# A linear attention's drain written out in an order of its own, with other banks for its output projections and a layer norm over two batches

## The reference

```
q = silu(causal_dwconv(h @ Wq, taps of 4)); k likewise        # h: layer-normed x
q, k = layernorm per head of 128, times weight, plus bias
v = h @ Wv; beta = sigmoid(h @ Wb + bb); gate = silu(h @ Wg)
per token t:  S = (1 - b_t) * S + b_t * (v_t outer k_t);  o_t = S q_t
x = x + (o * gate) @ Wo
x = x + ffn(layernorm(x))        # router, top 2 of 8, two silu layers, sums to rows 0..7
```

## Time and profile before

| what | value |
|---|---|
| runs | 1192.81, 1193.85, 1196.03 us, median 1193.85 |
| the profiled execution's own time | 1192.82 us |
| its span, first to last instruction | 1190.9 us |
| TensorE busy | 1132.6 us (95%) |
| VectorE, ScalarE, GpSimd busy | 929.5 (78%), 773.4 (65%), 635.5 us (53%) |
| mean granted clock of TensorE | 0.98 of 2.4 GHz |
| linear attention's drain | 1104 to 1148 us |
| last feed-forward layer | 1148 to 1190.9 us |

### The profile page before, as it was taken

How to read it: one execution, slowest core, us unless ns; L and a number is a source line. 1 busy time by engine, 2 the same in 40 slices (tenths; PEclk the granted TensorE clock), 3 DMA queues, 4 the chain that set the end, 5 groups by cost and what they waited for, 6 DMA issues and landing times. The chain is left out here.

```text
span 1190.9 us, 22446 instructions
## 1 busy us (share of the span) xinstructions
PE 1132.6 (95%) x7558; PEld 910.8 (76%) x7558; DVE 929.5 (78%) x2126; ACT 773.4 (65%) x1535; POOL 635.5 (53%) x1077
## 2 busy tenths in 40 slices
PE   8999999887998899999999999999999999999768
PEld 7443434336667799999999999999999999999646
DVE  6788887846558888888888888888888888888552
ACT  3367777673456777776777776777676777676423
POOL 4020500000705776877786777686777687767520
PEclk9899999998999999999999999999999999999889
DMA  6434434400220112112111110211110201010020
GB/s 182 55 55 56 55 55 56 55 2 6 110 69 20 49 33 82 34 47 68 47 33 48 67 48 32 83 32 48 67 48 32 83 32 47 32 48 33 16 71 1
DMA packets 23449, 60.50 MB, mean 51 GB/s; under 512 B 3367, under 2 KB 8359, under 8 KB 22183
## 3 DMA queue, kind: packets, MB, share of 16 engines
q1 hardware_dynamic: 23335, 59.07, 19.3%
HBM read 44.67 MB, written 2.33 MB: 39 GB/s over the span
## 5 line engine op out<-in xcount | busy, mean ns | idle before, releaser
L1714 DVE SCALAR_TENSOR_TENSOR ln_xn<-l_proj_q,par,ln_xn 128x511 f32<-128x511 f32 (+2 forms) x192 | 142.8, 744 | 98.5 <-ACT ln_xn L1613 96.2
L689 DVE TENSOR_REDUCE a_neg_max<-a_scores 128x1 f32<-128x512 f32 x244 | 155.1, 684 | 36.6 <-PE a_scores L417 34.8
L608 ACT ACTIVATE a_probs<-a_scores_t 128x512 f32<-128x512 f32 x256 | 138.5, 600 | 62.8 <-PE a_scores_t L436 61.8
L1619 ACT ACTIVATE ln_xn<-ln_xn,par 128x512 f32<-128x512 f32 x128 | 92.6, 723 | 92.6 <-DVE ln_xn L1714 92.6
L1370 POOL TENSOR_TENSOR l_k_tok<-l_normed,k_norm 128x384 f32<-128x384 f32 x64 | 65.1, 1017 | 156.6 <-ACT l_normed L1630 156.6
L1714 DVE SCALAR_TENSOR_TENSOR ln_xn<-l_proj_k,par,ln_xn 128x511 f32<-128x511 f32 (+2 forms) x192 | 143.4, 747 | 4.5
L1630 ACT ACTIVATE l_normed<-l_turn_q,l_shift,l_scale 128x128 f32<-128x128 f32 x256 | 96.3, 457 | 25.8 <-POOL l_shift L1362 25.8
L1360 POOL TENSOR_TENSOR l_scale<-l_small,l_minus_half 128x8 f32<-128x8 f32 x64 | 105.1, 1642 | 5.0
L1630 ACT ACTIVATE l_normed<-l_turn_k,l_shift,l_scale 128x128 f32<-128x128 f32 x256 | 97.1, 480 | 0.0
L1684 ACT ACTIVATE l_gate<-l_proj_gv 128x512 f32<-128x512 f32 x64 | 38.2, 597 | 80.7 <-PE l_proj_gv L1432 80.7
L1568 PE MATMUL l_outp<-l_masked,l_values 128*128 128x128 f32 x512 | 89.6, 277 | 0.1
(11 more groups left out here) (347 smaller groups left out, 3618.6 us busy)
## 6 DMA issues: line engine op xcount, KB each, us to landing
l_keep<-keep_rows SPq DMA_DIRECT2D x64, 448.0 KB, 3.6
a_stack<-a_dense SPq DMA_DIRECT2D x90, 128.0 KB, 5.1
head_raw<-w_heads SPq DMA_DIRECT2D x8, 1024.0 KB, 6.7
x_tok<-x SPq DMA_DIRECT2D x4, 512.0 KB, 8.6
wo_raw<-w_o SPq DMA_DIRECT2D x1, 2048.0 KB, 11.2
out<-x_tok SPq DMA_DIRECT2D x1, 1920.0 KB
a_stack<-a_max_rows_t SPq DMA_DIRECT2D x64, 4.0 KB
ctx_tok<-w_qkv SPq DMA_DIRECT2D x1, 768.0 KB, 7.0
```

The costliest lines, as they stand in the source:

```text
L608: act.activation(probs[:, n % 2, h, :], scores_t[(4 * n + h) % TURNS][:], ACT.Exp, scale=SOFT_SCALE).then_inc(probs_done, 1)
L689: dve.tensor_reduce(neg_max[:, g % 2, at:at + 1], max_bank(g, j), AX.X, ALU.max, negate=True).then_inc(max_done, 1)
L1619: act.activation(conv[:, w, m, :], conv[:, w, m, :], ACT.Silu, bias=par[:, h, 2 * TAPS + w:2 * TAPS + w + 1]).then_inc(act_sem[w], 1)
L1714: ins = dve.scalar_tensor_tensor(conv[:, w, m, s:], proj[w][:, 0:SEQ - s], par[:, h, tap:tap + 1], conv[:, w, m, s:], ALU.mult, ALU.add)
```

## The change

The steps for u = 0 to 63 keep their order and lose their conditions; stages that the drain needs become functions (`score_unit`, `sum_chunks`, `read_state`, `project_out`, `copy_state`, `add_out`, `token_statistics`, `mask`, `gate_out`, `decays`, and on GpSimd `late_rows` is split into `scaled_keys`, `decayed_queries` and `shifted_keys`). The drain's further steps are replaced on each engine by a function `drain`, a list in an order of its own. Token turns of unit 63 write `proj_q` and `proj_k` instead of the turn banks. Output projections of units 59, 60, 61 and 63 write `proj_gv`, that of unit 62 `scores`, instead of `outp`. The layer norm's work for batch 2 ends in the drain with its deviations; normalise, transposes, high and low parts of batch 2 are left to the feed-forward layer, as (3, 2) says.

```diff
+        LAST = UNITS - 1
+
+        def turn_bank(v, w):
+
+            return proj[w] if v == LAST else turn[w]
+
+        def out_bank(v):
+
+            if v < UNITS - 5:
+                return outp
+            return scores if v == LAST - 1 else proj_gv
...
+            def drain():
+                rows_in = 16 * NB * PAIRS
+                gated_low(LAST - 3, BODY - 4)
+                scaled_keys(LAST - 1)
+                scales(LAST, BODY - 1)
+                ln_d.deviations(pool, 0)
+                decayed_queries(LAST - 1, BODY - 2, rows_in)
+                shifted_keys(LAST - 1)
+                decayed(LAST - 1, BODY - 2)
+                scaled_keys(LAST)
+                shifted_keys(LAST)
+                decayed(LAST, BODY - 1)
+                gated_low(LAST - 2, BODY - 3)
+                decayed_queries(LAST, BODY - 1, rows_in)
+                ln_d.deviations(pool, 1)
+                gated_low(LAST - 1, BODY - 2)
+                gated_low(LAST, BODY - 1)
+                ln_d.deviations(pool, 2)
+
+            steps(step)
+            drain()
...
                 wait(pe, act_sem[w], v + 1)
-                wait(pe, qk_ready[w], v)
+                if v < LAST:
+                    wait(pe, qk_ready[w], v)
                 for t in range(TPB):
-                    last = pe.transpose(turn[w][:, t * P:(t + 1) * P], conv[:, w, k % 2, t * P:(t + 1) * P], ident[:])
+                    last = pe.transpose(turn_bank(v, w)[:, t * P:(t + 1) * P], conv[:, w, k % 2, t * P:(t + 1) * P], ident[:])
...
+            def read_state(v, k, sums, gates):
+
+                m, e, c = k % 2, k % 2, k // 2
+                wait(pe, masked_done, v + 1)
+                wait(pe, state_done, v + 1)
+                wait(pe, q_decayed, v + 1)
+                wait(pe, values_done, v + 2 - k % 2)
+                wait(pe, added, sums)
+                wait(pe, gated_done, gates)
...
+            def project_out(v, k, head):
+
+                w, half, bank = k // 2, k % 2, out_bank(v)
+                wait(pe, gated_lo_done, v + 2 - half)
+                for t in range(2):
+                    tok, j = slice((half * 2 + t) * P, (half * 2 + t + 1) * P), 0
+                    for e in range(2):
+                        r = (2 * w + e) % 4
+                        for lhs, rhs in split_passes(gated_hi[:, r, tok], gated_lo[:, r, tok],
+                                                     wo_hi[:, head + e, :], wo_lo[:, head + e, :]):
+                            last = pe.matmul(bank[:, t * D:(t + 1) * D], lhs, rhs, start=(j == 0), stop=(j == 5))
+                            j += 1
+                last.then_inc(out_done, 1)
...
                 if has(u, 5):
-                    v, kk = u - 5, (k - 5) % BODY
-                    w, half = kk // 2, kk % 2
-
-
-                    wait(pe, gated_done, min(v + 3, UNITS) if isinstance(v, int) else v + 3)
-                    wait(pe, gated_lo_done, v + 2 - kk % 2)
+
+                    v = u - 5
+                    wait(pe, gated_done, v + 3)
...
+            def drain():
+                head = 2 * (PAIRS - 1)
+                for w in range(2):
+                    turn_tokens(LAST, BODY - 1, w)
+                for w in range(2):
+                    turn_back(LAST - 1, w)
+                wait(pe, values_done, UNITS)
+                project_out(LAST - 4, BODY - 5, head)
+                score_unit(LAST - 1, BODY - 2)
+                read_state(LAST - 2, BODY - 3, LAST - 4, 0)
+                turn_back(LAST, 0)
+                sum_chunks(LAST - 1, BODY - 2)
+                turn_back(LAST, 1)
+                score_unit(LAST, BODY - 1)
+                ln_d.transpose(pe, 0, proj)
+                read_state(LAST - 1, BODY - 2, 0, LAST - 1)
+                sum_chunks(LAST, BODY - 1)
+                wait(pe, added, LAST - 3)
+                project_out(LAST - 3, BODY - 4, head)
+                read_state(LAST, BODY - 1, 0, LAST)
+                wait(pe, added, LAST - 2)
+                project_out(LAST - 2, BODY - 3, head)
+                ln_d.transpose(pe, 1, proj)
+                wait(pe, masked_done, UNITS)
+                project_out(LAST - 1, BODY - 2, head)
+                wait(pe, added, LAST - 1)
+                project_out(LAST, BODY - 1, head)
+
+            steps(step)
+            drain()
...
+            def drain():
+                gated_high(LAST - 3, BODY - 4)
+                norm_affine(LAST - 1, BODY - 2, 0)
+                norm_affine(LAST - 1, BODY - 2, 1)
+                normalise(LAST, BODY - 1, 0)
+                normalise(LAST, BODY - 1, 1)
+                copy_state(LAST - 1, BODY - 2)
+                norm_affine(LAST, BODY - 1, 0)
+                norm_affine(LAST, BODY - 1, 1)
+                gated_high(LAST - 2, BODY - 3)
+                ln_d.high_parts(act, 0, proj)
+                copy_state(LAST, BODY - 1)
+                gated_high(LAST - 1, BODY - 2)
+                gated_high(LAST, BODY - 1)
+                ln_d.high_parts(act, 1, proj)
+
+            steps(step)
+            drain()
...
+            def add_out(v, k):
+                n = batch_of(v) * TPB + 2 * (k % 2)
+                wait(dve, out_done, v + 1)
+                wait(dve, added, v - 2)
+                dve.tensor_tensor(x_tok[:, n:n + 2, :], out_bank(v)[:].rearrange("p (t d) -> p t d", t=2),
+                                  x_tok[:, n:n + 2, :], ALU.add).then_inc(added, 1)
...
-                if u in (UNITS + 2, UNITS + 4):
-                    ln_d.low_parts(dve, (u - UNITS - 2) // 2, proj)
-                if u in (UNITS + 1, UNITS + 3):
-                    ln_d.normalise(dve, (u - UNITS - 1) // 2)
-                if u in (UNITS, UNITS + 2, UNITS + 4):
-                    wait(dve, added, UNITS - BODY + 2 * ((u - UNITS) // 2 + 1))
-                    ln_d.statistics(dve, (u - UNITS) // 2)
...
+            def drain():
+                add_out(LAST - 5, BODY - 6)
+                token_statistics(LAST, BODY - 1)
+                wait(dve, added, UNITS - BODY + 2)
+                ln_d.statistics(dve, 0)
+                mask(LAST - 1, BODY - 2)
+                gate_out(LAST - 2, BODY - 3)
+                ln_d.normalise(dve, 0)
+                add_out(LAST - 4, BODY - 5)
+                decays(LAST, BODY - 1, 16 * NB * PAIRS)
+                carry(LAST - 1, BODY - 2)
+                mask(LAST, BODY - 1)
+                gate_out(LAST - 1, BODY - 2)
+                wait(dve, added, UNITS - BODY + 4)
+                ln_d.statistics(dve, 1)
+                carry(LAST, BODY - 1)
+                add_out(LAST - 3, BODY - 4)
+                ln_d.low_parts(dve, 0, proj)
+                gate_out(LAST, BODY - 1)
+                ln_d.normalise(dve, 1)
+                add_out(LAST - 2, BODY - 3)
+                wait(dve, added, UNITS - BODY + 6)
+                ln_d.statistics(dve, 2)
+                ln_d.low_parts(dve, 1, proj)
+                add_out(LAST - 1, BODY - 2)
+                add_out(LAST, BODY - 1)
 
             dve.wait_ge(consts_set, 2)
-            steps(step, 7)
-            ln_d.low_parts(dve, NB - 2, proj)
+            steps(step)
+            drain()
...
+        norm_and_ffn(nc, semaphore, "d", ffn, xn_hi, xn_lo, ident, x_tok, norm_tiles, ln_d, (NB - 1, NB - 2), out=out)
 
 
 def kernel(**inputs):
```

More of the change, by code:

```diff
@@ L1301, in has, with steps @@
             return not isinstance(u, int) or 0 <= u - lag < UNITS
-        def steps(step, lags):
+        def steps(step):
             for pair in range(PAIRS):
@@ L1330, in step @@
                     sp.dma_start(w_raw[:], w_heads[bass.ds(pair + 1, 1)]).then_inc(w_loaded, 16)
-            steps(step, 0)
+            steps(step)
         @block.gpsimd
@@ L1418, in step @@
                     low_weights(pair, of, k - SPLIT_AT[0])
-            steps(step, 4)
-            for g in range(1, NB - 1):
-                ln_d.deviations(pool, g)
+            def drain():
[18 more added lines that the diff above has]
+            drain()
         @block.tensor
@@ L1503, in expert_rows, with score_unit, sum_chunks @@
                 last.then_inc(rows_done, 1)
+            def score_unit(v, k):
+                for w in range(2):
+                    wait(pe, qk_ready[w], v + 1)
+                wait(pe, masked_done, v)
+                for t in range(TPB):
+                    last = score(t, k % 2)
+                last.then_inc(scored, 1)
+            def sum_chunks(v, k):
+                wait(pe, state_done, v)
+                wait(pe, k_decayed, v + 1)
+                wait(pe, values_done, v + 2 - k % 2)
+                for t in range(LATER):
+                    last = pe.matmul(chunks[:, t * DK:(t + 1) * DK], k_tok[:, t, :],
+                                     values[:, k // 2 % 2, t, k % 2 * DK:(k % 2 + 1) * DK], start=True, stop=True)
+                last.then_inc(chunks_done, 1)
@@ new lines, in read_state @@
+            def read_state(v, k, sums, gates):
```

(41 more changed lines are left out.)

180 lines of the change are left out of this document (61 added, 119 removed).

## The result

The changed kernel takes 1182.3 us (median of 5 runs, 1178.67 to 1184.77) where the kernel before takes 1193.66 in the runs beside it (5 runs, 1191.56 to 1196.03): a ratio of 0.9899, 95% interval [0.9873, 0.9925]. The forecast was 1181.8. A second series gave 1181.2, ratio 0.9911 [0.9882, 0.994]. The profiled execution took 1182.66 us with a span of 1180.8, so the span is 10.1 us shorter than before, where the sum said 12.0; the medians differ by 11.4.

The account below looks back on a forecast made before the run. The drain was taken as bound by a chain hopping between engines, the rest by TensorE. Gains 0.3 + 10.3 + 1.4 = 12.0 us took 1192.82 to 1180.8, plus 1.0 for the median: 1181.8 us, range 1177.5 to 1186 (8 in 10).

Parts of the forecast that it names:

- (a): Drain start: unit 63's token turns go first, so GpSimd's scales end at 1112.0 us, 2.4 us earlier.
- (b): GpSimd's queue behind the scales: chunk sums of unit 62 at 1116.0, head start eaten; VectorE's normalise collision costs 0.4 us.
- (c): TensorE's hole, 1110.1 to 1116.0: clock falls, back between 1119 and 1126; gain to unit 62's gate 0.3 us with (b).
- (d): Drain after the gate multiply of unit 62: chain of 11.5 us instead of 21.8, gain 10.3 us.
- (e): Feed-forward layer: batch 2's transposes cost 1.02 us, starting at the high clock gains 2.4; net gain 1.4 us.
- The bank waits: Old drain: TensorE's projections waited 1.9 and 1.8 us for the shared bank `outp`; these were to leave the chain.
- Rival 3: Drain not bound by order: new waits replace old ones one for one, time within 0.3%; chance 0.03.
- Rival 1: No low clock in the drain: gate of unit 62 2.5 to 3 us better, 1179 us; chance 0.15.
- rival 4: Slower: the hole leaves TensorE at 1.2 GHz for good, 1212 us; chance 0.03.
- Rival 2: GpSimd's queue replaces the bank; with longer low clock, gain 6 to 9 us, 1185 to 1188 us; chance 0.13.

Follow-up runs that it names:

- e6: Changed kernel with 52 unused identity transposes added on TensorE to fill its hole; 1179.03 us, ratio to the kernel before 0.9889.
- e7: Changed kernel with VectorE's normalise of batch 1 moved behind the statistics of batch 2; 1183.31 us, ratio to the kernel before 0.9912.
- e2: Changed kernel with batch 2's normalise, transposes, high and low parts put back in the drain; 1184.96 us, ratio to the kernel before 0.9917.
- e10: Kernel before with the new banks and batch 2's norm left to the feed-forward layer, old order kept; 1189.5 us, ratio 0.9975.
- e9: Changed kernel with projections in `outp` again and batch 2's norm back in the drain, leaving the order alone; 1185.63 us, ratio to the kernel before 0.9963.
- e4: Kernel before with only batch 2's normalise, transposes, high and low parts left to the feed-forward layer; 1190.0 us, ratio 0.9959.
- e3: Kernel before with only the new projection banks and their waits, order and norm as before; 1190.98 us, ratio 0.9983.
- e5: Changed kernel with GpSimd's first-batch deviations moved behind the decayed keys of unit 62; 1181.38 us, ratio to the kernel before 0.9897.

## Why the prediction was right

The forecast was 0.5 us from the median, and part of that closeness is luck. In the profiled executions, for which the sum was made, it was 1.9 us too hopeful (1180.8 foreseen, 1182.66 measured). I added 1.0 us, by which the median before lay above its profiled execution; after, the median lies 0.4 us below its own, and that made up for most of the miss. By its own steps, in the profiled execution:

- **(a) Token turns first.** Foreseen: first statistics at 1105.7, scales finished at 1112.0. Measured 1105.93 and 1112.28; TensorE's first drain instruction was itself 0.24 us later. Right.
- **(b) The queue behind the scales.** Foreseen: decayed keys at 1115.9, chunk sums at 1116.0; measured 1116.84 and 1116.95, so the head start was eaten as said, and 0.9 us more. Of these, 0.28 are the later scales. 0.35 are a slip in the sum: by its own rows (1.3 for the deviations, 2.95 from the start of the late queries to the end of the decayed keys, 1106.59 to 1109.54 in the kernel before) the four steps take 4.25 us, not 3.9. The last 0.3 are deviations and key steps that took longer than in these rows. The collision hit the other engine than I priced: GpSimd's key steps took 1.04 and 0.99 us, but VectorE's four normalises 3.25 for 1.38. The normalise's 1.9 us did not reach the gate, for which I had 0.4: VectorE waited 2.87 us for the scores behind it. By the Trainium skill (SBUF — State Buffer, Who interferes with whom) whoever issues first gets the ports that VectorE's fast modes share with GpSimd, for the whole instruction, and the other is blocked. By that the price was to be 1.4; the trace agrees in direction, as GpSimd's instruction was first at 1113.69 and VectorE's from 1113.75 on took 1.9 us longer.
- **(c) The clock.** Foreseen: a fall between 1112 and 1116, back between 1119 and 1126, gate at 1125.7. Measured: low from 1115.1 to 1125.3, gate at 1126.35. e6 shows the cause, and the price: from the start of the chunk sums to the gate the changed kernel takes 9.40 us and e6 6.27 (1116.27 to 1122.54), so the low clock costs 3.1, and 3.1 is what I had (1125.3 against 1122.2). The stretch was 10.2 us long, not 7, without costing more than that, as its first 1.8 us lay in the hole. So this step is right, and the gate is 0.65 us late for what stands in (b): chunk sums 0.95 late, less the 0.4 us of collision that did not come, plus 0.1. The gain of 0.3 us up to here became a loss of 0.3.
- **(d) After the gate of unit 62.** Foreseen 11.5 us, measured 12.75. From the gate of unit 63 on VectorE runs to the end without a break (the 0.42 us ahead of that gate stand where I had 0.2), and the last projection is done at 1137.75, before its add at 1138.42. The term that was mis-sized is the normalise of batch 1: 1.29 in the sum, 2.27 to the next start (2.35 long) in the trace, beside GpSimd's low part of unit 63, which is 1.0 of the 1.25 us. I had weighed this collision in (b) and not here. e7 shows that it is the collision, and that its removal alone wins nothing.
- **(e) The feed-forward layer.** Foreseen 1.4 us shorter, measured 42.79 - 41.37 = 1.42. The transposes take 1.02 us as said, the six router matmuls 1.55 for 2.72, the twelve upper ones 2.76 for 3.88. The layers of e2 and e10, in which the clock is low for 3.4 us near the start, are 0.7 and 1.6 us longer. That the clock is high there is not owed to the dense end alone: it was high in e9 with batch 2's norm in the drain, and fell in e10 without it.

The sum 0.3 + 10.3 + 1.4 = 12.0 became -0.3 + 9.0 + 1.4 = 10.1 us of span. Here 9.0 is 21.8 - 12.75, and the -0.3 stands for 1126.01 against 1126.35. The median moved 11.4 us; medians of so few runs differ by about a microsecond (1182.3 and 1181.2 for the same kernel).

As to what the gain comes from, the prediction named two things that left the old chain, batch 2's norm and the bank waits. The norm is shown, at 3.5 to 3.8 us of drain (e2, e4) for the some 5 that I gave. The bank waits aren't what they seemed: taken away alone they return as waits for GpSimd (e3), and it is the order that is worth 4.5 us by itself (e9), which the prediction didn't price apart. Rival 3 had this for the banks, and was wrong for the whole. Rival 1 needed a hole without a fall; rival 4's clock never stayed low. Rival 2's condition came true, the clock was low for longer than at 1119, but not its price: the last four projections all ran at the high clock. What it says of GpSimd's queue is so: ahead of the gate that queue is on the chain (e5).

## What to carry to other kernels

A wait for a shared buffer is worth only what is left when the engines' orders allow another buffer to be used: other banks brought nothing alone, and 1 to 2 us with the order. Work moved out of a sparse end into a dense stage shortens the end, and may be paid back again by the clock at which the next stage starts: with the norm moved, eight of nine profiled layers began with 18 matmuls at the high clock, with it in the drain one of four. Lay out both elementwise engines' queues side by side, and count every place where both work on SBUF, not only the first; then look for a hole in TensorE's work that one could fill, with real work first.

## What the runs showed that I had not expected

- Beside GpSimd's operations on 384 or 512 columns, VectorE's four normalises took 2.33 to 3.26 us for 1.35 to 1.38, and four scans with two inputs in SBUF took 2.87 (e6) where they otherwise take 1.35. GpSimd's decayed keys took 0.99 us for 0.83 beside the normalise.
- The low clock outlasted dense work: from 1117 to 1125 us TensorE was busy 7.08 of 8 us at a granted 0.50. In the kernel before the low stretch in the drain ended after 6.9 us.
- The anchor, behind the same instructions in every kernel, started between 1098.65 and 1109.14 us, with low stretches of the clock at other places each time. The runs of one kernel follow it: with the drain's code the same, the changed kernel took 1178.7 us at a mean granted clock of 0.986 and 1184.8 at 0.979. That is more than most parts of this change are worth, and is why the stages were compared from an anchor inside the kernel.
